# Unrolled VectorE rows, a moved transfer and two swapped GpSimd steps in an fp32-emulating MoE and LoRA kernel

## The reference

```python
# layer 0: B=8, S=512, H=256, I=1024, E=8 experts, 2 chosen for each sequence
rw = softmax(cond_8);  w, sel = top_k(rw, 2);  w = w / w.sum()
mlp(x, g, u, d) = (gelu_tanh(x @ g) * (x @ u)) @ d
y  = x + sum_over_chosen(w_e * mlp(x, gate_e, up_e, down_e)) + mlp(x, shared_gate, shared_up, shared_down)
# layer 1: R=16
out = y + y @ W_base.T + b_base + 2.0 * sum_e(cond_8[b, e] * (y @ A_e.T) @ B_e.T)
```

## Time and profile before

| | |
|---|---|
| median of 3 runs | 799.92 us (799.68 to 800.48) |
| the profiled execution | 800.2 us, of which 798.5 us from the first to the last instruction |
| PE busy | 790.7 us, 4277 matmuls |
| DVE busy | 653.6 us |
| ACT busy | 497.6 us |
| POOL busy | 311.5 us |
| granted TensorE clock | 1.00 of full over the whole span |
| transfers | 108.82 MB, 136 GB/s on the mean |

### The profile page before, as it was taken

One profiled execution on the slowest core, in us unless ns is written; L12 is line 12 of the kernel. 1 busy time (PEld: TensorE's weight loads), 2 busy tenths in 40 slices (PEclk: granted clock), 3 DMA queues, 4 the chain that ended last, 5 costly groups with the idle time before them and its releaser, 6 DMA issues.

```text
span 798.5 us, 14174 instructions
## 1 busy us (share of the span) xinstructions
PE 790.7 (99%) x4277; PEld 687.0 (86%) x4277; DVE 653.6 (82%) x874; ACT 497.6 (62%) x808; POOL 311.5 (39%) x308
## 2 busy tenths in 40 slices
PE   9999999999999999999999999999999999999998
PEld 7888888888888888889889888888998888898897
DVE  4866888888887788878978987888898789789787
ACT  5654564564664576766767666576675667666663
POOL 1531321321430355355344542634634443553441
PEclk9999999999999999999999999999999999999999
DMA  7426506304726742682664465277346526723400
GB/s 202 128 75 197 146 1 195 123 0 145 232 71 185 251 106 77 207 191 81 209 162 110 127 222 123 78 236 173 103 146 206 122 79 219 175 79 107 117 14 28
DMA packets 139894, 108.82 MB, mean 136 GB/s; under 512 B 63040, under 2 KB 131392, under 8 KB 139840
## 3 DMA queue, kind: packets, MB, share of 16 engines
q1 hardware_dynamic: 138688, 104.00, 43.4%
q0 software_dynamic: 1152, 4.19, 3.3%
HBM read 83.53 MB, written 24.64 MB: 135 GB/s over the span
## 4 chain that ended last, share of the span: by engine, by line
PE 89%; issue 4%; POOL 4%; DVE 1%; ACT 1%; POOLq 0%; DVEq 0%; ACTq 0%
PE ps_ring L859 55%; PE ps_acc L859 32%; POOL post L819 1%; POOL stage L805 1%; POOL stage L810 1%; POOL stage L808 1%; POOL stage L806 1%; DVE xc L1589 0%; PE ps_ring L981 0%; PE ps_acc L1075 0%; PE ps_acc L975 0%; DVE wide L1589 0%; PE ps_ring L880 0%; PE ps_ring L885 0%; PE ps_ring L889 0%
## 5 line engine op out<-in xcount | busy, mean ns | idle before, releaser
L859 PE MATMUL ps_ring<-xc,wide 128*128 128x512 f32 (+1 forms) x1854 | 385.6, 356 | 0.0
L859 PEld LDWEIGHTS ps_ring<-xc,wide 128*128 128x128 f32 x1854 | 317.0, 189 | 53.0 <-DVE post L1651 1.0
L1204 ACT CAST inner_hi<-post 128x512 fp32r<-128x512 f32 x192 | 116.2, 621 | 97.6 <-DVE post L1988 32.3
L859 PE MATMUL ps_acc<-inner_hi,wide 128*128 128x512 f32 x504 | 166.4, 390 | 0.0
L1589 DVE TENSOR_TENSOR inner_lo<-post,inner_hi 128x512 fp32r<-128x512 f32 (+1 forms) x145 | 136.4, 950 | 4.0 <-ACT inner_hi L1204 3.7
L1207 ACT ACTIVATE post<-post 128x256 f32<-128x256 f32 (+1 forms) x114 | 62.2, 558 | 99.9 <-DVE post L1912 70.6
L819 POOL TENSOR_TENSOR post<-post 128x256 f32<-128x256 f32 x78 | 82.0, 1071 | 91.4 <-ACT post L1456 91.4
L859 PEld LDWEIGHTS ps_acc<-inner_hi,wide 128*128 128x128 f32 x504 | 94.8, 188 | 18.9
L859 PE MATMUL ps_acc<-inner_lo,wide 128*128 128x512 f32 x252 | 98.5, 391 | 0.0
L859 PE MATMUL ps_acc<-inner_hi,sh_dn 128*128 128x512 f32 x256 | 83.9, 389 | 0.0
L740 POOL TENSOR_TENSOR post<-post 128x512 f32<-128x512 f32 x24 | 31.0, 1293 | 127.3 <-DVE post L1653 127.3
(11 more groups left out here) (127 smaller groups left out, 1067.5 us busy)
## 6 DMA issues: line engine op xcount, KB each, us to landing
rights_scratch<-xc SPq DMA_DIRECT2D x6, 1792.0 KB, 10.2
raw<-n_L_cond_skill_gate_dram SPq DMA_DIRECT2D x32, 256.0 KB, 3.0
raw<-in_L_cond_skill_up_dram SPq DMA_DIRECT2D x32, 256.0 KB, 3.6
raw<-n_L_cond_skill_down_dram SPq DMA_DIRECT2D x32, 256.0 KB, 3.9
xbuf<-n_L_cond_skill_gate_dram SPq DMA_DIRECT2D x32, 256.0 KB, 2.9
xbuf<-in_L_cond_skill_up_dram SPq DMA_DIRECT2D x32, 256.0 KB, 3.4
xbuf<-n_L_cond_skill_down_dram SPq DMA_DIRECT2D x32, 256.0 KB, 3.6
xt_scratch<-xbuf SPq DMA_DIRECT2D x8, 512.0 KB, 3.3
```

Source lines behind the costliest of these rows:

```text
L859: last = pe.matmul(dst, left_[a], right_[b], start=start and n == 0, stop=stop and n == len(PASSES) - 1, skip_group_check=adds)
L1204: return nc.scalar.copy(dst, src)
```

## The change

The eight rows of DVE are written out one after the other, so that its instruction stream has no branch and no computed semaphore values between the start and the end. On POOL the tokens' transfer moves behind C22 of step 12 (in the last row it stays where it was), and C22 of step 10 goes ahead of the sums for pair 7. Two waits for `acc0_out` and one for `layer1_landed` are dropped on DVE, and two pairs of half-size instructions in `layer1_constants` become one instruction each.

```diff
@@ POOL, row @@
                 sums_of_weights(b, 2)
                 ex_c22(b, 1)
-                add_tokens(b)
+                if last:
+                    add_tokens(b)
                 sums_of_weights(b, 3)
+
+                ex_c22(b, 2)
                 sums_of_weights(b, 4)
-                ex_c22(b, 2)
                 ex_c22(b, 3)
                 if not last:
+                    add_tokens(b)
                     sums_of_weights(b + 1, 0)
                 ex_c22(b, 4)
@@ DVE @@
             def acc1_to_stage(q):
-                if q > 0:
-                    dve.wait_ge(acc0_out, 2 * q)
                 dve.wait_ge(sh_down_done, 2 * PAIRS * (q + 1))
@@
             def layer1_constants():
-
-                dve.wait_ge(acc0_out, 2 * Q)
-                dve.wait_ge(layer1_landed, 6 * 16)
                 dve.wait_ge(a_hi, 1)
-                for half in (slice(0, P), slice(P, H)):
-                    last = take_lo(a_s[1][:, half], a_nat[:, half], a_s[0][:, half])
-                last.then_inc(a_ready, 1)
+                take_lo(a_s[1], a_nat, a_s[0]).then_inc(a_ready, 1)
                 dve.wait_ge(turned_w, 1)
                 V.tensor_copy(b_t[:], ps_misc[1][:, 0:H]).then_inc(b_t_done, 1)
-                for c in range(HC):
-                    last = V.tensor_copy(w_id[:, c * H:(c + 1) * H], ps_misc[0][:, c * H:(c + 1) * H])
-                last.then_inc(w_turned, 1)
+                V.tensor_copy(w_id[:], ps_misc[0][:]).then_inc(w_turned, 1)
@@
             row(0, 0, True, False)
-            row(1, 1, False, False, range(DVE_TURN_STEP))
-            with dve.Fori(0, (B - 2) // 2) as i:
-                row(i * 2 + 1, 1, False, False, range(DVE_TURN_STEP, K))
-                row(i * 2 + 2, 0, False, False)
-                row(i * 2 + 3, 1, False, False, range(DVE_TURN_STEP))
-            row(B - 1, 1, False, True, range(DVE_TURN_STEP, K))
+            for b in range(1, B):
+                row(b, b % 2, False, b == B - 1)
```

More of the change, by code:

```diff
@@ L64, in cond_resid_kernel @@
     TURN_STEP = 6
-    DVE_TURN_STEP = 8
     SEVEN = [1, 3, 5, 6, 7]
@@ L1922, in ex_rest_of, with row @@
                          gelu[1].rearrange("p (t n) -> p t n", t=2), ex_c2[:, :, HS:S])
-            def row(b, par, first, last, steps=range(K)):
+            def row(b, par, first, last):
                 split_at = SPLIT_FIRST if first else SPLIT_LATER
@@ L1948, in rest_of_x @@
                     take_lo(x_cur(1 - par, 1)[:, cols], xf[:, cols], x_cur(1 - par, 0)[:, cols]).then_inc(x_ready, 1)
-                for k in steps:
+                for k in range(K):
                     s = k // IC
```

## The result

The changed kernel takes 805.46 us (median of 6 runs, 805.23 to 805.8) against 799.8 us of the kernel before (6 runs beside it). The ratio is 1.007, 95% interval 1.0057 to 1.0083: 5.7 us slower, where 3.7 us less were forecast. The profiled execution has a span of 804.1 us; the granted clock is 1.00 in both.

The account below looks back on a forecast made before the run. PE, busy 790.7 of 798.5 us, was taken as the bound, with time lost mainly in two longer rows where DVE's loop turns. -4.44 - 0.13 + 0.84 = -3.73 took the median 799.92 to 796.2 us, range 794.8 to 799.0.

Parts of the forecast that it names:

- The tokens' transfer behind C22 of step 12: POOL, before the next row's first sums: 0.87 us of issue falls in idle time, cost 0.
- DVE without a loop: DVE at step 8: writing out rows removes both back branches and their issue gaps, gaining 2.49 + 1.95 = 4.44 us.
- C22 of step 10 ahead: POOL: sums for pair 7 delay DVE's split by 0.51; PE loses 0.84 us over 7 rows, row 0 gains 0.13.
- the neighbour row I chose for it: C22 of step 6, 1.76 us, beside a DVE low part; taken as the length of C22 of step 10.
- the margin of 0.39: Step 12: slack in us between DVE's L1897 plus hand-over and PE's seventh product, in an undisturbed row.
- Dropped waits and merged instructions: DVE's copies to `stage` and row 0 constants: some 0.1 us less each on an engine that then waits, 0.
- Past its break-even: Third rival: DVE's split over 0.98 us late by one more blocked POOL instruction, the change loses; 804.0 us, chance 0.07.

Follow-up runs that it names:

- the first experiment: The changed kernel with the tokens' transfer back in its old place behind C22 of step 6, all else the same; 795.34 us, ratio 0.9946.

## Why the prediction was wrong

**The step that failed** is the one headed "The tokens' transfer behind C22 of step 12", priced at 0: "the 0.87 lies in idle time". It lies there. I asked who on POOL is late behind the transfer, found C22 of step 14 with time to spare (POOL still waited 3.76 us before it), and didn't ask what DVE does while POOL's instructions follow the transfer. It measured +10.1 us (805.46 against 795.34). Row 2 of before did not warn of it: at step 6 a multiplication that started 0.52 us into the issue (416.01 and 0.87 us long) ran in its usual 0.49 us, but there no additions stood behind the transfer.

```profile
416.53 0.49 DVE L1875 SCALAR_TENSOR_TENSOR post<-post,coef_now 128x256 f32<-128x256 f32 x1
```

**DVE without a loop**, forecast -4.44: measured -4.6 (799.69 to 795.1). Right, in size and in mechanism.

**C22 of step 10 ahead**, forecast -0.13 + 0.84 = +0.71: measured -1.1 alone, and +0.2 with DVE unrolled, both near nothing. The mechanism of the lateness was right and its size too large. The split starts 9.01 us behind step 10's first product (438.76 against 429.75 in the changed kernel), in place of 8.87 (436.05 against 427.18): 0.14 late, not 0.51. The sums took the 3.47 us I gave them (435.18 to 438.65), but C22 took 1.46 and not 1.76, so the neighbour row I chose for it, with a DVE low part over its head, was too dear. With 0.14 the margin of 0.39 isn't used up and the 0.84 us fall away. Row 0 gains more than the 0.13 forecast: its period falls by 0.31 us with the swap alone. That the swap helps the turning rows I had left out of the sum, rightly, since the unrolling takes these away.

**Dropped waits and merged instructions**, forecast 0: no run has them alone. The kernel with DVE unrolled lacks them and has its first like product at 252.90; the first experiment has them and is at 252.97, and its total is no less. Nothing contradicts the 0.

**The rivals.** "Past its break-even" gave 804.0 and was near in number, with a chance of 0.07 and for the wrong cause: the sums for pair 7 did not become the bound. The Trainium skill's "SBUF — State Buffer", section "Who interferes with whom", was weighed at C22 alone. It says that a VectorE instruction with two SBUF inputs and a GpSimd one that reads SBUF exclude each other, and that the later one waits for the other. The runs agree with the exclusion, and differ in how long: behind a transfer the multiplication waited for three additions, not one.

**Accounting**, from the first to the eighth like product in the profiled executions: 490.32 before, 485.90 with DVE unrolled (-4.42), 485.92 with C22 ahead too and the transfer in its old place (+0.02), 496.26 in the changed kernel (+10.34, on the mean 1.48 for each of seven rows). With the transfer behind the sums it is 485.55; the difference from 485.92 is the one period of 67.17 us in the first experiment, for which I have no cause.

**What stays open**: why POOL's additions keep running behind a transfer. The multiplications that were kept out, those of step 12 and in one kernel that of step 10, all arrived 0.27 to 0.41 us behind the start of the first addition and ended 0.3 us after the end of the third. There POOL stands still for the first time, since the fourth addition needs the third's result. Whether the standstill lets DVE in, or the third addition in itself, no run parts. That POOL's instructions pile up during the issue and so leave no gap would fit, and was not shown.

## What to carry to other kernels

When a step moves on one engine, look also at the engine that was seen to be kept out by it (here DVE by POOL), and at what that one does at the new time, not only at who is late behind the step. A transfer that GpSimd issues should stand where GpSimd waits next, not ahead of a run of its additions beside VectorE's two-input work. A hardware loop on an engine whose slack is less than what a turn costs (here 0.5 us against up to 2.75) is worth writing out if the program's size allows it.

## What the runs showed of the hardware

- Behind a transfer issued by POOL, a two-input VectorE instruction was kept out over three additions: 2.35 us for one that takes 0.47, nearly the same for a quarter of the transfer (longest 2396 ns), and 2051 ns for a plain copy.
- Among additions without a transfer ahead, VectorE got in after one: 0.64 us for the same multiplication, arriving at the same moment.
- Directly behind the same transfer and with no additions the multiplication took 0.47 us.
- A turn of DVE's loop cost 2.24 and 2.75 us of idle time on that engine and 1.95 and 2.49 us of the span; in a kernel whose rows were delayed already the idle time was 1.55 and 1.60 us.
